# Linear attention and expert mixing: a new order of TensorE's work in each batch, the last addition put behind the last division, the sums of the last four batches as products with ones, and narrower filler products

## The reference, cut to what matters

```
def _L1_xattn_ref(query, key, value, attention_mask, Wq, bq, Wk, bk, Wv, bv, Wqf, Wkf, Wo, bo):
    # NH = 16 heads of HD = 16, FD = 64 features
    q = heads(query, Wq, bq); k = heads(key, Wk, bk); v = heads(value, Wv, bv)
    q_prime = relu(einsum('bhnd,fd->bhnf', q, Wqf))
    k_prime = relu(einsum('bhnd,fd->bhnf', k, Wkf)) * attention_mask[:, None, :, None]
    kv = einsum('bhnf,bhne->bhfe', k_prime, v)
    qkv = einsum('bhmf,bhfe->bhme', q_prime, kv)
    qk_sum = einsum('bhmf,bhf->bhm', q_prime, sum(k_prime, axis=2))
    return (qkv / (qk_sum + 1e-08)) @ Wo.T + bo

def _L1_ffn_ref(hidden_states, sim_matrix, gates, w_q, w_k, w_v, o_weights):
    # each batch: mean over tokens -> similarity to 32 experts -> routing, mask (of 16 batches)
    # one mixed value matrix and one mixed output matrix per batch, then two products with x
x = x + _L1_xattn_ref(_layernorm(x), ctx_2048, ctx_2048, mask, ...)
x = x + _L1_ffn_ref(_layernorm(x), ...)
```

## Time and profile before

| | us |
|---|---|
| median of 3 runs | 977.67 (977.49 to 978.47) |
| the profiled execution, its own time | 976.68 |
| its span, first to last instruction | 974.9 |
| TensorE busy in the span | 934.1 (96%) |
| VectorE, ScalarE, GpSimd busy | 627.8, 475.5, 239.0 |
| mean granted clock of TensorE | 0.995 of full |

### The profile page before, as it was taken

The page is one execution under the profiler, slowest core; times in us unless marked ns, Lnnn a source line. Parts: engine busy times, 40 slices in busy tenths (PEclk is TensorE's granted clock), DMA queues, the critical chain, the costliest instruction groups (busy, mean ns, idle before and its releaser), DMA issues.

```text
span 974.9 us, 19976 instructions
## 1 busy us (share of the span) xinstructions
PE 934.1 (96%) x7621; PEld 793.7 (81%) x7621; DVE 627.8 (64%) x1383; ACT 475.5 (49%) x1593; POOL 239.0 (25%) x257
## 2 busy tenths in 40 slices
PE   7999999999999999999999999999999999999877
PEld 5777777899788888888888888888888887677657
DVE  6678887797875576564556454556456665777854
ACT  3877876444445554444344444434444554443431
POOL 3455786572011111111111010111111212110000
PEclk9999999999999999999999999999999999999989
DMA  8100000002330000000000000100010004000002
GB/s 304 38 2 3 2 2 2 2 1 90 108 152 1 1 1 2 1 1 2 1 1 2 1 1 1 44 18 1 1 58 30 1 1 176 1 2 2 2 1 87
DMA packets 10941, 27.89 MB, mean 29 GB/s; under 512 B 1824, under 2 KB 6976, under 8 KB 10208
## 3 DMA queue, kind: packets, MB, share of 16 engines
q1 hardware_dynamic: 10128, 26.41, 7.6%
q10 hardware_dynamic: 720, 0.20, 0.1%
HBM read 24.51 MB, written 2.10 MB: 27 GB/s over the span
## 4 chain that ended last, share of the span: by engine, by line
PE 84%; DVE 8%; ACT 4%; issue 2%; DMA 0%; POOL 0%; SPq 0%; DVEq 0%; ACTq 0%; POOLq 0%
PE bank L50 15%; PE bank L52 14%; PE bank L51 14%; PE bank L2035 6%; PE bank L1984 5%; PE bank L392 3%; PE bank L402 3%; PE bank L2025 3%; PE bank L1899 2%; PE bank L1908 2%; PE bank L414 2%; PE bank L1041 2%; PE bank L178 2%; PE bank L1031 2%; PE bank L1017 2%
## 5 line engine op out<-in xcount | busy, mean ns | idle before, releaser
L1845 POOL TENSOR_TENSOR wa_prob<-wa_prob,wa_rsum 128x512 f32<-128x512 f32 x64 | 67.5, 1055 | 405.2 <-DVE wa_rsum L2418 405.2
L2217 ACT ACTIVATE wa_prob<-wa_prob,wa_negmax 128x128 f32<-128x128 f32 x256 | 99.7, 390 | 66.3 <-DVE wa_negmax L2407 66.1
L50 PE MATMUL bank<-norm_xT_hi,wide_hi 128*128 128x512 f32 x256 | 106.0, 414 | 0.2 <-DVE norm_xT_lo L189 0.2
L51 PE MATMUL bank<-norm_xT_lo,wide_hi 128*128 128x512 f32 x256 | 101.0, 395 | 0.0
L52 PE MATMUL bank<-norm_xT_hi,wide_lo 128*128 128x512 f32 x256 | 101.0, 395 | 0.0
L2474 DVE TENSOR_TENSOR wa_z_lo<-bank,wa_z_hi 128x512 fp32r<-128x512 f32 x64 | 44.2, 691 | 86.9 <-ACT wa_z_hi L2251 86.4
L583 ACT ACTIVATE v_prob<-bank,la_negmax 128x128 f32<-128x128 f32 x256 | 91.1, 399 | 1.1 <-DVE la_negmax L661 1.1
L2225 ACT COPY wa_q<-bank 128x512 f32<-128x512 f32 x64 | 37.6, 587 | 93.6 <-PE bank L52 93.6
L2232 ACT COPY wa_v<-bank 128x512 f32<-128x512 f32 x64 | 37.3, 584 | 89.6 <-PE bank L52 89.6
L329 POOL TENSOR_TENSOR v_prob<-v_prob,la_rsum 128x512 f32<-128x512 f32 x64 | 66.5, 1041 | 51.8 <-DVE la_rsum L666 51.7
L173 POOL TENSOR_TENSOR norm_rstd<-norm_rstd,minus_half 128x4 f32<-128x4 f32 x23 | 24.6, 1069 | 206.1 <-DVE norm_rstd L133 175.2
(11 more groups left out here) (277 smaller groups left out, 2372.0 us busy)
## 6 DMA issues: line engine op xcount, KB each, us to landing
wide_raw<-in_wide_w SPq DMA_DIRECT2D x16, 512.0 KB, 6.8
em_w<-in_em_w SPq DMA_DIRECT2D x1, 4096.0 KB, 13.3
x<-in_x SPq DMA_DIRECT2D x4, 512.0 KB, 4.9
lc_kt<-in_ctx_rev SPq DMA_DIRECT2D x1, 2048.0 KB, 10.7
lc_toep<-in_toeplitz SPq DMA_DIRECT2D x1, 2048.0 KB, 14.5
li_kt<-in_ctx_rev SPq DMA_DIRECT2D x4, 512.0 KB, 6.6
out_x<-x SPq DMA_DIRECT2D x8, 256.0 KB, 2.9
w_or_y<-in_l_w SPq DMA_DIRECT2D x1, 1024.0 KB, 6.3
```

The costliest lines, as they stand in the source:

```text
L50: nc.tensor.matmul(out, a[0], b[0], start=start, stop=False, skip_group_check=True)
L51: nc.tensor.matmul(out, a[0], b[1], start=False, stop=False, skip_group_check=True)
L1845: nc.gpsimd.tensor_tensor(prob[:, s], prob[:, s], rsum[:, s, :].unsqueeze(2).to_broadcast([P, G, P]), ALU.mult).then_inc(prob_ok, 1)
L2217: last = nc.scalar.activation(prob[:, s, j, :], prob[:, s, j, :], ACT.Exp, bias=negmax[:, s, j:j + 1], scale=SCALE, accum_out=sums[:, s, j ...
```

## The change

Four things are changed, all behind the wide attention:

1. In linear attention a list `AHEAD` picks batches 1, 2, 4, 5, 6, 8, 9, 10 and 12, 13, 14. There `early(n)` moves from behind the query features to just behind the key features, ahead of `project(n - 1)`, and on ScalarE the copy that empties its bank moves ahead of `keep_den`. In batches 0, 3, 7 and 11 it is `values(n + 2)` that moves there. Batch 15 keeps its order.
2. In batch 15 the addition of batch 14 comes behind the division of batch 15. The last projection writes another bank (4), and so no longer waits for earlier additions.
3. The token sums of the last four batches are made by TensorE: eight products of a 128 x 128 piece of the normalised x with a column of ones, into bank 6; VectorE copies the eight columns instead of reducing two banks. ScalarE's copies of the transposes wait for the transposes alone.
4. The filler products have 512, 512, 128, 128, 128 and 128 columns instead of four times 512.

```
+    AHEAD = [n in (*MIX_AT.values(), SIM_AT) or G * 3 > n > 0 and n % G < 3 for n in range(NB - 1)] + [False]
+    def out_bank(n):
+        return (b_kv if n < NB - 1 else banks[4])[:, 0:D]
...
         def project(n):
             reached(pe, o_ok, n + 1)
-            reached(pe, kv_ok, min(n + 2, NB))
-            wait(pe, x_ok, n)
+            if n < NB - 1:
+                reached(pe, kv_ok, n + 2)
+                wait(pe, x_ok, n)
...
             if n + 1 < NB:
                 key_features(n + 1)
+            if AHEAD[n]:
+                early(n)
+            elif n + 2 < NB:
+                values(n + 2)
             if 0 < n < NB - 1:
                 project(n - 1)
             numerators_and_denominators(n)
...
-            early(n)
-            if n + 2 < NB:
+            if not AHEAD[n]:
+                early(n)
+            elif n + 2 < NB:
                 values(n + 2)
             late(n)
...
+            if AHEAD[n]:
+                keep_early(n)
+            keep_den(n)
+            if t < NG and j >= 2:
+                keep_query_features(t, j - 2)
+            if not AHEAD[n]:
+                keep_early(n)
...
-            if n > 0:
+            if 0 < n < NB - 1:
                 update(n - 1)
             divide(n, chain)
+            if n == NB - 1:
+                update(n - 1)
...
+        def tail_sum(j):
+            for c in range(DC):
+                last = nc.tensor.matmul(self.tail_rep()[:, c, j:j + 1], self.xn[:, j, c * P:(c + 1) * P],
+                                        self.ones[:, 0:1], start=True, stop=True, skip_group_check=True)
+            return last
+        reached(pe, self.const_ok, 1)
         reached(pe, self.s_xn, 1)
...
         last.then_inc(self.s_tr.sem, 1)
+        for j in range(3):
+            tail_sum(j)
         reached(pe, self.s_xn, 2)
+        tail_sum(3).then_inc(self.rep_tail.sem, 1)
...
-        for m in range(4):
-            nc.tensor.matmul(banks[0], self.w[:, 0, m * P:(m + 1) * P], self.w[:, 0, 0:512], start=True, stop=True)
+        for m, width in enumerate((512, 512, P, P, P, P)):
+            nc.tensor.matmul(banks[0][:, 0:width], self.w[:, 0, m * P:(m + 1) * P], self.w[:, 0, 0:width], start=True,
+                             stop=True)
...
-        reached(act, self.rep_tail, 1)
+        reached(act, self.s_tr, 1)
...
-        reached(dve, self.s_tr, 1)
-        nc.vector.tensor_reduce(self.rep[:, :, NB - G:NB - 1], early.rearrange("p c (b t) -> p c b t", b=3), AX,
-                                ALU.add).then_inc(self.rep_tail.sem, 1)
-        reached(dve, self.s_tr, 2)
-        nc.vector.tensor_reduce(self.rep[:, :, NB - 1], late, AX, ALU.add).then_inc(self.rep_tail.sem, 1)
+        reached(dve, self.rep_tail, 1)
+        nc.vector.tensor_copy(self.rep[:, :, NB - G:NB], self.tail_rep()).then_inc(self.rep_tail.sem, 1)
```

More of the change, by code:

```diff
@@ L1037, in project @@
             reached(pe, o_ok, n + 1)
-            reached(pe, kv_ok, min(n + 2, NB))
-            wait(pe, x_ok, n)
+            if n < NB - 1:
+                reached(pe, kv_ok, n + 2)
+                wait(pe, x_ok, n)
             for c in range(DC):
-                last = nc.tensor.matmul(b_kv[:, 0:D], o[:, n % 2, c, :], w32[:, O, c, :], start=(c == 0),
+                last = nc.tensor.matmul(out_bank(n), o[:, n % 2, c, :], w32[:, O, c, :], start=(c == 0),
                                         stop=(c == DC - 1))
@@ L1121, in tensor_program @@
                 key_values(n + 1)
+        reached(pe, kf_ok, NB)
         project(NB - 1)
-        reached(pe, kf_ok, NB)
         reached(pe, kv_ok, NB)
@@ L1189, in scalar_program, with keep_early @@
         keep_key_values(0)
-        for n in range(NB):
+        def keep_early(n):
             g, j = divmod(n, G)
             t = g + 1
-            keep_den(n)
-            if t < NG and j >= 2:
-                keep_query_features(t, j - 2)
             if t < NG and j == 0 and g > 0:
@@ L1204, in scalar_program @@
                 mix.scalar_sim(act, b_p)
+        for n in range(NB):
+            g, j = divmod(n, G)
+            t = g + 1
+            if AHEAD[n]:
[5 more added lines that the diff above has]
+                keep_early(n)
             if t < NG and j == 0:
@@ L1270, in update @@
             reached(dve, o_ps, n + 1)
-            nc.vector.tensor_tensor(x[:, n, :], b_kv[:, 0:D], x[:, n, :], ALU.add).then_inc(x_ok.sem, 1)
+            nc.vector.tensor_tensor(x[:, n, :], out_bank(n), x[:, n, :], ALU.add).then_inc(x_ok.sem, 1)
         chain = Chain(dve, chain_s.sem, 0, NB, chain_s.base)
@@ L1477, in tail_banks, with tail_rep @@
         return psum[:, 2:4, 0:3 * P], psum[:, 5, 0:DC * P].rearrange("p (c t) -> p c t", c=DC)
+    def tail_rep(self):
+        return self.pr.banks[6][:, 0:DC * G].rearrange("p (c b) -> p c b", c=DC)
     def v_banks(self, n):
@@ L1525, in tensor_program @@
         last.then_inc(self.s_tr.sem, 1)
-        reached(pe, self.const_ok, 1)
         reached(pe, self.sim_ok, 1)
@@ L1603, in scalar_program @@
         early, late = self.tail_banks()
-        reached(act, self.rep_tail, 1)
+        reached(act, self.s_tr, 1)
         nc.scalar.copy(self.xT[:, :, NB - G:NB - 1, :], early.rearrange("p c (b t) -> p c b t", b=3))\
             .then_inc(self.kept.sem, 1)
-        reached(act, self.rep_tail, 2)
+        reached(act, self.s_tr, 2)
         nc.scalar.copy(self.xT[:, :, NB - 1, :], late).then_inc(self.kept.sem, 1)
@@ L1627, in vector_program @@
         best, left, small = self.best, self.left, self.small
-        early, late = self.tail_banks()
         chain = Chain(dve, self.chain_s.sem, 0, 12, self.chain_s.base)
-        reached(dve, self.s_tr, 1)
-        nc.vector.tensor_reduce(self.rep[:, :, NB - G:NB - 1], early.rearrange("p c (b t) -> p c b t", b=3), AX,
-                                ALU.add).then_inc(self.rep_tail.sem, 1)
-        reached(dve, self.s_tr, 2)
-        nc.vector.tensor_reduce(self.rep[:, :, NB - 1], late, AX, ALU.add).then_inc(self.rep_tail.sem, 1)
+        reached(dve, self.rep_tail, 1)
+        nc.vector.tensor_copy(self.rep[:, :, NB - G:NB], self.tail_rep()).then_inc(self.rep_tail.sem, 1)
         reached(dve, self.kept, 3 * DC)
```

## The result

The changed kernel takes 980.87 us (median of 15 runs, 978.61 to 983.62), the kernel before 977.67 (15 runs, 975.94 to 979.64). The ratio is 1.0027, with a 95% interval of 1.0018 to 1.0036. The forecast of 980.8 us hits the median closely, but not all its terms do: two missed and made up for each other, which is luck.

The account below looks back on a forecast made before the run. TensorE was taken to set the pace in linear attention. New waits of 10.5 us against 6.5 removed give +4.0, sums 0, fillers -0.9: +3.1 on 977.67, so 980.8 us, range 977.2 to 983.3.

Parts of the forecast that it names:

- ReLU copies: Key features two batches after 3, 6, 7, 10, 11 wait for ScalarE's copies to free shared banks: 3.3 us new.
- transposing bank: Early transposes in batches 13 and 14 wait for ScalarE's copies of the previous batch's second transpose: 2.8 us new.
- second low part: Queries passes of batches 1, 5 and 9 wait for VectorE's low part of x, second half: 3.2 us new.
- first low part: Keys passes in batches 4 and 8 wait for the low part of x, first half: 0.9 us new.
- the rest: Batch 15's numerators and key-value sums wait longer, made late by the other waits: 0.3 us new.
- Removed: 6.5 us: Old waits gone in linear attention: 3.9 us ahead of projections, 2.2 at banks and transposes, 0.4 at the last projection.
- its work stays the same: Linear attention: TensorE, busy 111.5 of 122 us, sets the pace, so only its idle time changes.
- last division: Batch 15: the last projection finds its division done earlier, ahead of batch 14's addition: 0.4 us gained.
- I take the middle, 0: Tail: 16 one-column loads and products on TensorE, between a gain of 0.7 us and a loss of 0.5, 2.3 at half clock.
- the bound for half clock: Tail sums: at 0.113 us each at full clock, the 16 take 3.6 us at half clock, a loss of 2.3.
- Fillers: Tail: three quarters of the filler columns take 5.04 us instead of 5.95, 0.9 us less.
- The rival of the clock in the mixing: Tail: narrower fillers end before the clock rises, mixing runs partly at half clock, up to 3.4 us more, 984; chance 0.08.

Follow-up runs that it names:

- order_values_back: Kernel before with only the new order, but in batches 3, 7 and 11 the values stand behind the query features again: 981.50 us, ratio 1.0041.
- best: Changed kernel with early work ahead only in batches 2, 4, 8, 12, values ahead in 6 and 10, sums back on VectorE: 971.98 us, ratio 0.9948.
- passes_only: Kernel before with only the early work put ahead in batches 1, 5, 9, 13 and 14: 980.43 us, ratio 1.0023.
- best_two: As best_warm, but early work ahead in batches 2, 5, 9 and 12 instead of 2, 4, 8 and 12: 972.16 us, ratio 0.9945.
- order_only: Kernel before with only the new order of the batches on TensorE and ScalarE: 980.35 us, ratio 1.0038.
- best_warm: As best, with two more filler products of 512 columns in the idle stretch behind the last addition: 971.90 us, ratio 0.9942.
- after_warm: Changed kernel with two more filler products of 512 columns in the idle stretch behind the last addition: 979.82 us, ratio 1.0025.
- end_only: Kernel before with only the last division put ahead of the addition and the last projection into another bank: 976.84 us, ratio 1.0001.
- no_sums: Changed kernel with the token sums back on VectorE: 979.88 us, ratio 1.0028.
- sums_warm: Kernel before with only the sums on TensorE and two more 512-column fillers behind the last addition: 977.06 us, ratio 1.0010.

## Why the prediction was right, and where it was not

**Where the loss would come from: right.** That TensorE's order trades short gaps for longer waits at ReLU copies, low parts and the transposing bank is what the trace shows, at each place that was named, and at the key features of batch 5 too, which are in the prediction's sum but not in its list of signs. The new waits measure 10.6 us start against start, where 10.5 were forecast: ReLU copies 3.3 (3.3), second low part 3.1 (3.2), first low part 0.9 (0.9), transposing bank 3.0 (2.8), the rest 0.3 (0.3). The ReLU copies' part is the 3.42 us from query features to key features, which stand at all five places in the changed trace, less the work that is left between them. The numerators of batch 15 wait 1.36 us before the change, not 1.32. The cause is shown by experiment for the ReLU copies (order_values_back, and best's batch 6). For batches 5 and 9 the place and the releaser were right, but the cause lay one batch ahead: passes_only and best_two removed the wait by leaving batches 4 and 8 alone. For batches 13 and 14 no run moved the transposes by themselves.

**What the order would take away: mis-sized.** "Removed: 6.5 us" failed; it is about 8.5, as the stage grew by 2.1 and not by 4.0. The step behind it is "its work stays the same": the work itself got shorter by what stands ahead of it. A projection takes 1.03 or 1.04 us from start to start behind key features with a wait, 1.06 without one, and 0.95 or 0.96 behind a pass, values or transposes (881.31 to 882.26 above); in thirteen batches that is 1.0 us. A keys pass that need not wait takes 1.48 instead of 1.59, and the transposes behind the old bank waits gained in the same way: 0.8 us together, and the last division (next paragraph) 0.2.

The rows of the weight loads, of batch 7 before and of batch 8 in the changed kernel, show the difference:

```profile
871.24 0.73 PEld L1041 LDWEIGHTS bank<-h_or_w,li_o 128*128 128x128 f32 x4 [0.40 <-issue]
```

```profile
881.08 0.84 PEld L1046 LDWEIGHTS bank<-h_or_w,li_o 128*128 128x128 f32 x4
```

Before, the first load starts 0.03 us ahead of the projection's first product (871.27); behind a pass it starts 0.23 ahead (881.31). In batches 1 to 14 of both traces, where the numerators follow, the projections with a load 0.11 to 0.23 us ahead take 0.95 or 0.96 us, and those with 0.04 or less take 1.03 to 1.06. That is the revised theory in order_only's expectation; no run tested it by itself.

**The last division: mis-sized**, 0.64 instead of 0.4 us. The last projection now follows the transposes without a stop.

**Sums: wrong.** "I take the middle, 0" failed, and so did the prediction by one of its own signs, "if the sums take over 2 us": they took 3.21. The interval is 2.75 us longer in the changed kernel's profile, 0.4 beyond the bound for half clock. Some 0.7 of that is not the sums': in order_only and passes_only, whose clock was also at half from the transposes on, the interval is 5.71 and 5.70 with VectorE's reductions, 0.67 more than before. In the chain the six transposes take 1.52 us in the changed kernel (936.18 above) and 0.86 before, which the bound had left out:

```profile
933.16 0.86 PE bank L1520 x6
```

Against these two runs the sums cost 2.1 us at half clock, and against best_warm 0.56 at full: near the two upper bounds, 2.3 and 0.5, and far from the middle. The nearer row was the mixing products.

**Fillers: right in kind.** -0.9 was forecast; -1.2 in the changed kernel, -0.6 alone, according to when the clock rises. (The row, 0.53 on average from 940.80 to 940.90, puts the rise before at 940.89 and not at 940.84; the term stays 0.9.) The rival of the clock in the mixing did not come with the change as it stands, where the clock is still low when the fillers start. It came in two of the four executions with two more fillers (after_warm and best_two), not by fillers that end too soon for the rise, but with the idle time behind them.

**What was missing:** the clock inside the stage. Four of the profiles with a long wait in the stage show a fall behind it (end_only, order_values_back, after_warm, no_sums), at 1.5 to 1.6 us each. The kernel before has two such waits (both in batch 15) and the changed one six. The mean granted clock that is on record for each execution says how much of the difference may go with the clock, though not where it was low: the profiles at 0.995 have about 7 us at half from 815 us on, those at 0.993 about 10.5. The kernel before was at 0.995 in 56 of 78 executions (median 976.98 us), the changed one in 3 of 15 (979.26); at 0.993 the medians are 979.1 (10 executions) and 981.03 (11). At equal clock the change costs about 2 us, and the rest of the 3.2 goes with its lower clock. The three executions are few, and why the clock was low in so many is not shown.

So the sum, 4.0 + 0 - 0.9, came out right by luck: the stage was forecast 1.9 us too long, the interval 2.75 too short and the fillers 0.3 too long, and time at half clock in the stage was not counted at all.

## What to carry to other kernels

Filling a gap with work from further down the queue pays only if that work was not itself covering a longer wait: for each piece moved, check the interval that it leaves (here 3.42 us from query features to the shared banks) before the one that it fills. Decide it batch by batch: the rule for all batches made the stage 2.8 us longer, where a choice among them, with the end of the change, made it 3.3 us shorter. And a column sum as a product with ones is not cheap for streaming one column only: here the 16 loads of the 128 x 128 pieces were the price, 1.7 us at full clock and 3.2 at half.

## What the hardware showed that was not expected

- The granted clock fell to half behind single waits of TensorE of 1.3 to 1.5 us between dense work (at 827.2, 913.4, 925.8 and 926.8 in four profiles), and not behind the same waits in others, the changed kernel's own profile among them. It stayed low to 830.6, 916.8, 929.2 and 930.2, though TensorE was busy again. So the wait alone does not decide it, and what else does is open. In sums_warm it fell inside the fillers, 1.2 us behind a wait of 0.37 us.
- The same products take different times by what stands ahead of them: a projection 0.95 or 0.96 us behind wide products or transposes and 1.03 to 1.06 behind key features, a keys pass 1.48 us in a stream and 1.59 behind a short wait. The first load of weights stands 0.11 to 0.23 us ahead of the first product in the short projections of batches 1 to 14 and 0.04 us or less in the long ones.
- A float32 product of one column with 128 x 128 loaded shows two loads and two products, 0.106 us for each pair at full clock and 0.2 at half.
